# One norm for two, expert gates spread on the chip, and attention layers ended by query halves

## The chip, the cores and the metric

The kernel runs on one core of one Trainium2 chip. The metric is the device time of one execution in microseconds (us); less is better. Five engines work side by side: TensorE (PE; its weight loads are PEld), VectorE (DVE), ScalarE (ACT), GpSimd (POOL) and SyncE (SP), which here only issues DMAs.

## The reference

A stream of 1024 tokens of width 128 passes two layers. Each layer is an attention block over a context of 6404 rows (16 heads of 64), then a block of 8 experts of which each token takes two.

```python
x = x + tanh(g_xattn[0]) * L0_xattn(ctx, layernorm(x), ...)   # normalises its latents once more
x = x + tanh(g_ffn[0])   * L0_ffn(layernorm(x), ...)          # relu experts, 512 wide
x = x + tanh(g_xattn[1]) * L1_xattn(layernorm(x), ctx, ...)   # "stable" norm in and out
x = x + tanh(g_ffn[1])   * L1_ffn(layernorm(x), ...)          # gelu experts, 64 wide

def stable_layernorm(x, g):
    x = x / max(x, axis=-1)
    return (x - mean(x)) * rsqrt(var(x) + 1e-5) * g
```

In layer 0 the attention takes `layernorm(x)` and applies a layer norm with weights to it again. In layer 1 the input is `stable_layernorm(layernorm(x))`, and the attention output passes `stable_layernorm` once more. So both attention inputs are two norms in a row.

## The kernel before

Tokens lie in `X` as 8 tiles of 128 rows. An attention layer runs 8 groups (`NG`) of 2 heads (`GH`). In a group the context comes in chunks of tiles. For each chunk both query halves (n = 0 and 1, 512 queries each) are worked: `score` (PE), `exp` (ACT), `p_low` (DVE, the low part of the probabilities), `mix_high`, `mix_low` and `mix_last` (PE). After a chunk's half, `add_out` (DVE) adds the accumulated output, 128x512 for each of two heads, into `oacc`. Row 127 of `oacc` holds the softmax denominators. The very last unit of the loop is half n = 1 of the last chunk; half n = 0 of `oacc` is complete one unit, some 10 us, earlier.

The order of the work is written out by hand: each engine runs its own program in order, and semaphores join them. A group's output is finished in the group after it, in the shade of the loop: `load_den` (SP) writes the denominator row to DRAM, reads it back spread over partitions, `sum_inverse` (DVE) inverts it, and SP writes it out and broadcasts it into `den`. `o_high` (ACT) and `o_low` (DVE) split `oacc` in two parts, `final` (PE) multiplies by the output weights in four quarters f (head e = f // 2, half n = f % 2), `final_mul` (DVE) applies `den`, `final_add` adds into `YT`. For the eighth group (r = `NG`) there is no loop left, and the same steps run behind it.

After that a second `nc.Block()` turns `YT` back to token rows and adds it to `X`; in layer 1 it divides by the row maximum and applies `layer_norm` first. A block ends with all engines meeting.

The start of layer 1 on PE is in this order: `project_kv(0, 0)`, `transpose_k(0, 0)`, `project_kv(0, 1)`, and only then the transposes of the normed tokens, which wait for `lat_ready`. `project_kv(0, 0)` waits for `wkv_low(0)`, which is DVE work, and DVE's program has it between the first statistics and the first `ln_apply`.

In the last expert block (`moe_layer`, L = 1) `combine` (DVE) makes the gates with tokens on partitions. `turn_combine` (PE) turns them, `save_combine` (SP) writes them to DRAM, and eight DMAs read them back, each row broadcast to 64 partitions of `spread`. DVE multiplies `hid` by `spread`, and PE projects with the result as stationary operand.

## Time and profile before

| | us |
|---|---|
| median of 3 runs | 4258.66 (4256.95 to 4258.74) |
| the profiled execution | 4258.93 |
| its span, first to last instruction | 4257.1 |
| PE busy | 4085.8 (96%) |
| DVE busy | 3369.8 (79%) |
| ACT busy | 3159.8 (74%) |
| mean granted TensorE clock | 0.983 of full |

The span is 1.8 us shorter than the execution's own time. The page's slices of 106 us show PE busy by nine tenths or more in nearly all; the slices at the start, in the middle and at the end, where one layer gives over to the next, show less.

### The profile page before, as it was taken

Reading aid. Unit: us, or ns where it says so; the run is one execution under the profiler, and the core shown is the slowest. Engines: PE = TensorE matmul, PEld = TensorE weight load, DVE = VectorE, ACT = ScalarE, POOL = GpSimd, SP = SyncE. Lnnn points to the kernel's source line nnn. Section 1 sums busy time; section 2 is a strip of 40 time slices with the busy share of each in tenths; the row PEclk is TensorE's granted clock in tenths of the full one; section 3 lists DMA queues with packets and bytes.
Section 4 is the critical chain, followed back from the end, with each engine's and each line's share of the span. In section 5 each row is a group of like instructions: output and inputs, shape, how many; then the busy total and the mean of one; then the engine's idle time right before and its main releaser. Section 6 shows DMA issues by size and latency. Waiting matters only on the chain. (4 is left out here: it accounts for less than half of the span.)

```text
span 4257.1 us, 66053 instructions
## 1 busy us (share of the span) xinstructions
PE 4085.8 (96%) x26167; PEld 2647.6 (62%) x26167; DVE 3369.8 (79%) x5206; ACT 3159.8 (74%) x5109; POOL 412.3 (10%) x333
## 2 busy tenths in 40 slices
PE   4999999999999999999989899999999999999996
PEld 3666666666666666666657666666666666666664
DVE  7878888788887888878867778777877777877775
ACT  5888898888988889888854666676767676666662
POOL 4111111111111111111100000000000000000000
PEclk8999999999999999999989899999999999999997
DMA  1000000000000000000012000000000000000001
GB/s 41 1 1 17 1 17 1 1 17 1 17 1 1 17 1 17 1 1 18 1 52 79 1 1 17 1 17 1 17 1 17 1 5 13 1 17 1 15 1 44
DMA packets 30550, 50.24 MB, mean 12 GB/s; under 512 B 9166, under 2 KB 19414, under 8 KB 28182
## 3 DMA queue, kind: packets, MB, share of 16 engines
q1 hardware_dynamic: 28324, 45.85, 3.5%
q8 instruction: 211, 3.46, 0.3%
q14 instruction: 93, 0.76, 0.1%
q10 hardware_dynamic: 1922, 0.17, 0.0%
HBM read 45.15 MB, written 0.85 MB: 11 GB/s over the span
## 5 line engine op out<-in xcount | busy, mean ns | idle before, releaser
L819 DVE TENSOR_TENSOR a_probs_lo<-a_probs 128x1024 fp32r<-128x1024 f32 x1760 | 2126.5, 1222 | 562.2 <-ACT a_probs L595 254.6
L591 ACT ACTIVATE a_probs<-scores_ps,a_c_bias,a_k_rstd 128x512 f32<-128x512 f32 x1888 | 1311.9, 776 | 31.3 <-PE scores_ps L1248 30.8
L1273 PE MATMUL out_ps<-a_probs_lo,a_v 128*128 128x512 f32 x3520 | 1134.4, 443 | 0.0
L1266 PE MATMUL out_ps<-a_probs,a_v 128*128 128x512 bf16 x3520 | 952.5, 390 | 17.6 <-DVE a_out_acc L832 17.6
L595 ACT ACTIVATE a_probs<-scores_ps,a_c_bias 128x1024 f32<-128x1024 f32 x816 | 867.6, 1112 | 114.0 <-PE scores_ps L1248 113.3
L1273 PEld LDWEIGHTS out_ps<-a_probs_lo,a_v 128*128 128x128 f32 x3520 | 658.0, 188 | 218.6
L1248 PE MATMUL scores_ps<-a_q_hi,a_k_hi 64*128 64x512 f32 x3520 | 790.4, 444 | 3.1 <-ACT a_probs L591 1.6
L1248 PE MATMUL scores_ps<-a_q_lo,a_k_hi 64*128 64x512 f32 x3520 | 700.9, 392 | 0.0
L1248 PE MATMUL scores_ps<-a_q_hi,a_k_lo 64*128 64x512 f32 x3520 | 697.3, 390 | 0.0
L1266 PEld LDWEIGHTS out_ps<-a_probs,a_v 128*128 128x128 f16 x3520 | 272.2, 96 | 560.5 <-issue 303.0
L560 ACT ACTIVATE a_v<-proj_ps 128x256 f16<-128x256 f32 x448 | 172.2, 384 | 488.9 <-PE proj_ps L1171 488.6
L487 POOL TENSOR_TENSOR a_k_rstd<-a_k_stat,minus_half 128x4 f32<-128x4 f32 x240 | 322.3, 1343 | 1617.4 <-DVE a_k_stat L796 1617.4
L1248 PEld LDWEIGHTS scores_ps<-a_q_hi,a_k_hi 64*128 64x128 f32 x3520 | 332.1, 184 | 192.6 <-issue 87.6
L832 DVE TENSOR_TENSOR a_out_acc<-out_ps,a_out_acc 128x512 f32<-128x512 f32 x576 | 370.4, 685 | 80.5 <-PE out_ps L1273 79.3
L1248 PEld LDWEIGHTS scores_ps<-a_q_lo,a_k_hi 64*128 64x128 f32 x3520 | 335.1, 185 | 74.2
L1248 PEld LDWEIGHTS scores_ps<-a_q_hi,a_k_lo 64*128 64x128 f32 x3520 | 334.7, 186 | 37.4
L571 ACT ACTIVATE a_k_hi<-proj_ps 128x256 fp32r<-128x256 f32 x448 | 172.3, 385 | 238.2 <-PE proj_ps L1179 237.8
L1171 PE MATMUL proj_ps<-a_wkv_hi,a_x_hi 128*128 128x256 f32 x896 | 260.0, 290 | 28.3 <-DVE a_k_lo L811 16.8
L1256 PE MATMUL spare_ps<-a_probs,a_v_last 128*32 128x512 bf16 x3520 | 282.1, 394 | 0.0
L577 ACT ACTIVATE a_v<-a_v 128x512 fp32r<-128x512 f16 x448 | 280.5, 626 | 0.0
L1171 PE MATMUL proj_ps<-a_wkv_lo,a_x_hi 128*128 128x256 f32 x896 | 254.6, 284 | 0.0
L1171 PE MATMUL proj_ps<-a_wkv_hi,a_x_lo 128*128 128x256 f32 x896 | 252.3, 282 | 0.0
(299 smaller groups left out, 3286.2 us busy)
## 6 DMA issues: line engine op xcount, KB each, us to landing
a_den<-a_inv_row SPq DMA_DIRECT2D x16, 1024.0 KB, 4.9
normed<-in_L_xattn_we_g SPq DMA_DIRECT2D x16, 256.0 KB, 2.7
m_gate_spread<-m_combine_row SPq DMA_DIRECT2D x8, 512.0 KB, 4.1
a_wkv_raw<-in_L_xattn_wkv_g SPq DMA_DIRECT2D x16, 128.0 KB, 2.0
a_wo_raw<-in_L_xattn_wo_g SPq DMA_DIRECT2D x16, 128.0 KB, 2.0
m_w_raw<-in_L_ffn_w1T SPq DMA_DIRECT2D x8, 256.0 KB, 4.2
m_w_raw<-in_L_ffn_w2T SPq DMA_DIRECT2D x8, 256.0 KB, 4.7
m_gate_spread<-m_combine_row SPq DMA_DIRECT2D x8, 256.0 KB, 5.5
```

Of the source, the lines that this page charges most:

```text
L487: nc.gpsimd.tensor_tensor(krs[:, par, 2 * j:2 * j + 2, :].rearrange("p t h -> p (t h)"), kst[:, 1, :], mhalf[:, 0:2 * GH], ALU.pow).then_i ...
L571: nc.scalar.activation(kh[:, par, 2 * j:2 * j + 2, :], proj[:, 0:2 * P].rearrange("p (t k) -> p t k", k=P), ACT.Copy).then_inc(hi_done, 1)
L577: nc.scalar.activation(v32[:, par, 2 * j:2 * j + 2, :, :].rearrange("p t h k -> p (t h) k"), v16[:, par, 2 * j:2 * j + 2, :, :].rearrange( ...
L591: ins = nc.scalar.activation(probs[:, pb, e * 512:(e + 1) * 512], scores[:, b, e * 512:(e + 1) * 512], ACT.Exp, bias=cbias[:, tile:tile + ...
L595: ins = nc.scalar.activation(probs[:, pb, :], scores[:, b, :], ACT.Exp, bias=cbias[:, 1:2] if last else cbias[:, 0:1])
L819: nc.vector.tensor_tensor(plow[:, idx % NPL, :], probs[:, idx % NB, :], p_hi[:, idx % NB], ALU.subtract).then_inc(plo_ready, 1)
L832: ins = nc.vector.tensor_tensor(oacc[:, e, q], outs[:, e * 512:(e + 1) * 512], oacc[:, e, q], ALU.add)
L1171: last = nc.tensor.matmul(dst, a[:, x], w[:, :].rearrange("p (a c) -> p a c", a=2), start=t == 0 and m == 0, stop=m == 2, skip_group_check ...
L1248: last = nc.tensor.matmul(scores[:, b, e * 512:(e + 1) * 512], kk[r, c % 2, t, :], qq[r, n * 512:(n + 1) * 512], start=m == 0, stop=m == 2)
L1256: last = nc.tensor.matmul(last_ps[j:j + 32, :], vlast[:, c % 2, t, e, 4 - 4 * n:36 - 4 * n], p_hi[:, idx % NB, e * 512:(e + 1) * 512], sta ...
L1266: nc.tensor.matmul(outs[:, e * 512:(e + 1) * 512], v16[:, c % 2, t, e, :], p_hi[:, idx % NB, e * 512:(e + 1) * 512], start=t == 0, stop=False)
L1273: nc.tensor.matmul(outs[:, e * 512:(e + 1) * 512], v32[:, c % 2, t, e, :], plow[:, idx % NPL, e * 512:(e + 1) * 512], start=False, stop=t ...
```

## The change

1. `ln_stats` gets `twice`: in layer 0 the two norms become one, with the variance v replaced by v (1 + eps) + eps². The second statistics, its power on POOL and the second `ln_apply` go.
2. `max_norm` (new) does a layer norm and the division by the maximum as one: it works out the statistics and the maximum of the unchanged rows, and one factor from both. At the start of layer 1 it replaces norm, maximum, division and second norm; it now stands before `wkv_low(0)` and `wq_low(0)` on DVE. At the end of layer 1 it replaces the division and `layer_norm`.
3. The first addition into `YT` becomes a copy (with the bias in layer 0), so POOL no longer clears `Y`.
4. The end of the eighth group goes by halves. For half 0 the denominators take the way through DRAM as before, but of 512 queries and from the moment when half 0 of `oacc` is complete. For half 1, PE takes them out of `oacc` as columns (eight products with eight columns of the identity), DVE inverts the columns, eight transposes spread them over partitions into `outs`, and ACT copies them to `den`. The output weights are split before the last two pairs of the loop. The quarters run in the order f = 0, 2, 1, 3. The closing block is gone; its work stands at the end of the first one, and each half is turned back as soon as it is summed.
5. The last expert block widens the gates on DVE (parts 0, 3) and ACT (parts 1, 2) to `wide`, PE transposes them into PSUM, and DVE multiplies from there in halves. Nine DMAs go. The projection writes to `scores[:, 1]`, after all four transposed parts.

```diff
-            nc.vector.tensor_scalar(stat[:, 3, c + a:c + b], part[:, a:b, 7], LN_EPS, None, ALU.add).then_inc(var_ready, 1)
+        def max_norm(dve, step, x3, dst3, part, var_ready, rstd_ready, n):
+            x, dst = tiles_of(x3), tiles_of(dst3)
+            ln_moments(dve, step, x, 0, QT, part)
+            top, inv, sq = (stat[:, i, 0:QT] for i in range(3))
+            step(nc.vector.tensor_reduce(top, x3[:, :, :], AX.X, ALU.max))
+            step(nc.vector.tensor_tensor(sq, top, part[:, 0:QT, 6], ALU.subtract) if x3 is X else
+                 nc.vector.tensor_copy(sq, top))
+            step(nc.vector.reciprocal(inv, sq))
+            step(nc.vector.tensor_tensor(sq, inv, inv, ALU.mult))
+            step(nc.vector.tensor_tensor(sq, sq, part[:, 0:QT, 7], ALU.mult))
+            nc.vector.tensor_scalar(stat[:, 3, 0:QT], sq, LN_EPS, None, ALU.add).then_inc(var_ready, 1)
+            dve.wait_ge(rstd_ready, n)
+            step(nc.vector.tensor_tensor(stat[:, 0, 0:QT], stat[:, 0, 0:QT], inv, ALU.mult))
+            ln_apply(dve, step, x, dst, 0, QT, part, rstd_ready, n)
...
 # layer 1, start, DVE
-                    ln_stats(dve, lstep, tiles_of(X), 0, QT, B["few"], var_ready)
                     constants()
+                    max_norm(dve, lstep, X, Y, B["few"], var_ready, rstd_ready, 1)
+                    prep_steps.append(lstep.n)
+                    dve.sem_inc(lat_ready, 1)
                     wkv_low(0)
                     wq_low(0)
...
 # end of an attention layer, DVE
+                        if g == NG - 1 and i == NPR - 1:
+                            wo_low(NG)
+                            sum_inverse_half()
+                            for e in range(GH):
+                                o_low_half(0, e)
                         if i in ENDS:
                             add_out(g, s0, *ENDS[i][0])
...
+                o_low_half(1, 0)
+                column_inverse()
+                o_low_half(1, 1)
+                for n in range(2):
+                    for f in (n, 2 + n):
+                        final_mul(NG, f, last_no(f))
+                    for f in (n, 2 + n):
+                        final_add(NG, f, last_no(f))
...
 # the same, PE
+                for f in (0, 2):
                     final(NG, f, None)
+                for e in range(GH):
+                    pe.wait_ge(o_added, NG * NADD + e + 1)
+                    for j in range(4):
+                        last = nc.tensor.matmul(proj[:, (4 * e + j) * 8:(4 * e + j + 1) * 8], oacc[:, e, 512 + j * P:512 + (j + 1) * P],
+                                                ident[:, P - 8:P], start=True, stop=True, skip_group_check=True)
+                    last.then_inc(d_col, 1)
+                final(NG, 1, None)
+                pe.wait_ge(d_inv, 1)
+                for e in range(GH):
+                    for j in range(4):
+                        last = nc.tensor.transpose(outs[:, k * P:(k + 1) * P], inv8[:, k:k + 1].broadcast_to([P, P]), ident[:, :])
+                    last.then_inc(d_spread, 1)
+                final(NG, 3, None)
...
 # the last expert block, PE
+                    hidden(0)
+                    hidden(1)
+                    spread(0)
+                    hidden(2)
+                    spread(1)
+                    hidden(3)
+                    pe.wait_ge(gelu_done, 3)
+                    spread(2)
+                    pe.wait_ge(hg_done, 2)
+                    spread(3)
+                    pe.wait_ge(gelu_done, 4)
```

## Rows read from the trace of the kernel before

**Rows 1.** Layer 1's loop: stretch, PE, PEld, DVE, ACT, POOL busy (x), clock, DMA.
```profile
2400.00:4170.00 1770.00, 1763.19 (x11498) 1131.98 (x11496) 1387.70 (x1911) 1211.17 (x1715) 10.89 (x14) 1.00 0.03 8
```

**Rows 2.** The chain that ended last, its last two pieces: start, us, what.
```profile
4243.49 10.13 PE out_ps L1869 x64
...
4253.64 0.69 DVE residual L1845
```

**Rows 3.** Timeline of DVE at the start: start, us, engine, line, operation, tiles.
```profile
20.01 1.65 DVE L126 BATCH_NORM_STATS2 squares<-normed 128x6 f32<-128x128 f32 x8
...
22.48 0.06 DVE L997 MEMSET a_c_max<- 128x1 f32 x1
...
24.36 2.14 DVE L139 TENSOR_SCALAR normed<-normed,squares,stat 128x128 f32<-128x128 f32 x8 [0.21 <-POOL stat L151]
```

**Rows 4.** Timeline of layer 1's start on DVE, ACT and PE.
```profile
2338.99 0.29 DVE L837 TENSOR_TENSOR a_wkv_lo<-a_wkv_raw,a_wkv_hi 128x128 fp32r<-128x128 f32 x1 [0.95 <-ACT a_wkv_hi L602]
...
2341.63 0.38 ACT L562 ACTIVATE normed<-proj_ps 128x256 f32<-128x256 f32 x1
...
2347.18 0.41 DVE L805 SCALAR_TENSOR_TENSOR a_v<-a_v,proj_ps 128x252 f16<-128x252 f16 x1
...
2349.32 0.58 PE L1171 MATMUL proj_ps<-a_wkv_hi,a_x_hi 128*128 128x256 f32 x1 [0.93 <-DVE a_k_lo L811]
...
2351.43 1.97 PE L1322 MATMUL scores_ps<-identity,branch 128*128 128x128 f32 x8 [0.46 <-DVEq L1080]
```

**Rows 5.** Timeline of DVE at the end of layer 1's attention.
```profile
4171.81 1.29 DVE L832 TENSOR_TENSOR a_out_acc<-out_ps,a_out_acc 128x512 f32<-128x512 f32 x2 [0.59 <-PE out_ps L1273]
...
4177.63 2.36 DVE L819 TENSOR_TENSOR a_probs_lo<-a_probs 128x1024 fp32r<-128x1024 f32 x2 [1.12 <-ACT a_probs L595]
4181.73 1.29 DVE L832 TENSOR_TENSOR a_out_acc<-out_ps,a_out_acc 128x512 f32<-128x512 f32 x2 [1.75 <-PE out_ps L1273]
...
4186.49 0.48 DVE L849 SCALAR_TENSOR_TENSOR a_wo_lo<-a_wo_raw,a_lift_col,a_wo_hi 128x256 fp32r<-128x256 f32 x1
...
4193.31 2.48 DVE L937 TENSOR_TENSOR a_den<-scores_ps,a_den 128x512 f32<-128x512 f32 x4 [6.17 <-DMA a_den<-a_inv_row]
...
4200.58 1.42 DVE L1428 COPY normed<-scores_ps 128x512 f32<-128x512 f32 x2 [2.38 <-PE scores_ps L1411]
...
4203.53 1.22 DVE L1432 TENSOR_TENSOR normed<-normed,stat 128x1024 f32<-128x1024 f32 x1
```

**Rows 6.** The page's DMA issues: count, KB each, us from issue to landing.
```profile
a_den<-a_inv_row SPq DMA_DIRECT2D x16, 1024.0 KB, 4.9
...
m_gate_spread<-m_combine_row SPq DMA_DIRECT2D x8, 512.0 KB, 4.1
```

**Rows 7.** As rows 1, for four microseconds in layer 1's tail.
```profile
4184.00:4188.00 4.00, 0.77 (x2) 0.70 (x3) 3.00 (x4) 2.46 (x5) 0.00 (x0) 0.54 0.02 2
```

**Rows 8.** Timeline of PE: four transposes at the full clock.
```profile
2333.41 0.66 PE L1783 MATMUL scores_ps<-identity,branch 128*128 128x128 f32 x4 [0.67 <-DVE branch L1667]
```

**Rows 9.** Timeline of DVE at the end of layer 0's attention.
```profile
2193.10 2.57 DVE L819 TENSOR_TENSOR a_probs_lo<-a_probs 128x1024 fp32r<-128x1024 f32 x2 [0.97 <-ACT a_probs L591]
2196.87 1.29 DVE L832 TENSOR_TENSOR a_out_acc<-out_ps,a_out_acc 128x512 f32<-128x512 f32 x2 [1.21 <-PE out_ps L1273]
...
2216.47 1.54 DVE L1425 SCALAR_TENSOR_TENSOR residual<-scores_ps,gates,residual 128x512 f32<-128x512 f32 x2 [2.12 <-PE scores_ps L1411]
```

**Rows 10.** Timeline of the last expert block on DVE, ACT and PE.
```profile
4232.03 0.25 DVE L1524 TENSOR_SCALAR m_combine<-m_combine,gates 128x64 f32<-128x64 f32 x1
...
4233.45 1.02 ACT L1827 ACTIVATE m_hidden<-scores_ps 128x1024 f32<-128x1024 f32 x1 [1.23 <-PE scores_ps L1863]
...
4235.08 1.88 PE L1863 MATMUL scores_ps<-normed_T,m_w 128*128 128x512 f32 x4
```

**Rows 11.** PE's instructions of L1869 alone, two stretches: busy, weight loads, clock, DMA.
```profile
4244.00:4248.00 4.00, 4.00 (x21) 4.00 (x20) 0.50 0.96 207
4249.00:4252.00 3.00, 3.00 (x28) 3.00 (x28) 0.97 0.00 0
```

More of the change, by code:

```diff
@@ L121, in flamingo, with ln_moments @@
         few = sqz[:, :, :].rearrange("p t d -> p (t d)")[:, 0:8 * QT].rearrange("p (t k) -> p t k", k=8)
-        def ln_stats(dve, step, x, a, b, part, var_ready, c=0):
+        def ln_moments(dve, step, x, a, b, part):
             for t in range(a, b):
@@ L766, in _ @@
                                 wo_split(g)
+                        if g == NG - 1 and i == NPR - 3:
+                            wo_split(NG)
                         if g < NG - 1:
@@ new lines, in _ @@
+                pe.wait_ge(lo_done, ONE + NG * NI)
+                for e in range(GH):
+                    pe.wait_ge(o_added, NG * NADD + e + 1)
[4 more added lines that the diff above has]
+                final(NG, 1, None)
@@ new lines, in _ @@
+                pe.wait_ge(d_inv, 1)
+                pe.wait_ge(o_added, 2 + NG * NADD)
+                for e in range(GH):
+                    for j in range(4):
+                        k = 4 * e + j
+                        last = nc.tensor.transpose(outs[:, k * P:(k + 1) * P], inv8[:, k:k + 1].broadcast_to([P, P]), ident[:, :])
+                    last.then_inc(d_spread, 1)
+                final(NG, 3, None)
+                for n, dst in enumerate((last_ps, proj)):
+                    pe.wait_ge(f_add, 4 * (NG - 1) + 2 * n + 2)
+                    for t in range(4):
+                        last = nc.tensor.transpose(dst[:, t * P:(t + 1) * P], YT[:, (4 * n + t) * P:(4 * n + t + 1) * P], ident[:, :])
+                    last.then_inc(tr_done, 1)
@@ L1856, in _, with hidden @@
                     router(pe)
-                    for k in range(FC):
+                    def hidden(k):
                         if k >= 2:
                             pe.wait_ge(gelu_done, k - 1)
-                        if k == 3:
-                            turn_combine(pe)
                         for c in range(2):
```

203 lines of the change are left out of this document (110 added, 93 removed).

## Prediction

> **What bounds the kernel now.** I read the page first, for shares and slices, then a table by stretch. In a layer's loop PE is busy for all but 0.4% at the full clock [rows 1]; the change leaves the instructions there as they are but for the last three pairs of the eighth group. So what can be won lies in the seams: the two starts, the two tails and the last expert block, where short steps follow one another over engines and PE mostly waits. I then read each seam's timeline on all engines, since a seam gains only by what its own chain of waits gives up. The chain that ended last shows just the end: the projection of the last experts and the addition after it [rows 2].
>
> A measurement here can tell about 0.2%, 8.5 us, from no change. The sum is made against the profiled execution's 4258.93 us, which is 0.3 above the median of the runs.
>
> **Start of layer 0.** DVE's second statistics begin at 20.01 and end before 22.48; then, after 0.21 us of waiting for POOL, the second application takes 2.14 us [rows 3]. Both go: 2.46 + 0.21 + 2.14 = 4.8 us. DVE works nearly without a break here and the rest of its program follows as before, PE's transposes come right after it, and the context rows had landed by then, so I take all 4.8 as gain. The bounds are 3.5, if a later piece turns out to wait for a load, and 5.3.
>
> **Start of layer 1.** DVE loses a whole norm. The new one is statistics, maximum, five small steps, POOL's power and one application: I get its end at 2344.3, where the old second one ended at 2351.3. That looks like 7 us, and I take nothing of it. `project_kv(0, 0)` waits for `wkv_low`, which moves behind `max_norm`: from 2338.99 to 2344.4. From there PE, ACT and DVE must alternate. From the start of `wkv_low` to the end of ACT's read of the first keys it took 2338.99 to 2342.01, 3.0 us; `v_low` then takes 0.5 (before, DVE did it only at 2347.18, because it was held by the norms); and from the end of `v_low` at 2347.59 to the free PE behind `project_kv(0, 1)`, which starts at 2349.32 and has 1.65 us of products, 3.4 us went by [rows 4]. Sum: 2344.4 + 3.0 + 0.5 + 3.4 = 2351.3. PE's program has the transposes of the tokens behind that; they began at 2351.43 [rows 4]. So they begin where they began. What DVE was late for, PE's order is late for next. Gain 0.1, bounds -1 and +1.5.
>
> **Tail of layer 1, before.** The loop's last products end at 4181.9. DVE adds them until 4183.0, and the copies of the turned result end at 4202.0 [rows 5]. Between stand the splits, 16 products on a PE whose clock had fallen (0.54 granted from 4184 to 4188, mostly the 1.2 GHz level, after PE stood idle) [rows 7], the denominators' way through DRAM, the eight passes of multiplication and addition (2.48 for four, so 0.62 each), a block's end and eight transposes.
>
> **Tail of layer 1, after.** Half 0 of `oacc` is complete at 4173.1, and its sums are back long before DVE ends its last `p_low` at 4180.0 [rows 5]. Then DVE does, in order, `wo_low` (0.48), the reciprocal (0.25) and two half splits (0.62 each), to 4182.0; only then the last `add_out`, 0.3 late, to 4183.3; `o_low_half(1, 0)` to 4183.95. PE goes from its last product straight to f = 0 and 2 (eight products, 1.9 us at the full clock), sixteen instructions for the columns (1.95, bounded by a full transpose's 0.13 each [rows 8] above and 0.9 in all below), f = 1 (0.95), eight transposes (1.1) and f = 3: it ends at 4188.9 and never stands idle long, so I keep the full clock. The column inverse is done at 4186.05, and behind it, on DVE, waits `o_low_half(1, 1)`, to 4186.75.
>
> The broadcast of half 0's inverses can leave at 4182.6 (reciprocal, two small stores with their landing of 1.4 us). It is half of the 1024 KB that take 4.9 us to land; another broadcast, of 512 KB, took 4.1 [rows 6]. I take 4.1, as the size is the same: 4186.7, where DVE comes free anyway. The eight passes end at 4186.75 + 8 x 0.62 = 4191.75; the copy of half 0 (0.71) is done while PE turns half 1 (0.66 [rows 8]), and the second copy ends at 4193.25. Gain 4202.0 - 4193.25 = 8.75.
>
> The Trainium skill speaks against the idea that half the bytes take half the time: its page DMA: Bandwidth & Descriptors, section Anatomy of one DMA, puts a fixed cost of about 2.0 us on each DMA whatever its size. The rows agree that it is far from half (4.9 against 4.1). By that page an estimate for the half is 2.0 + (4.9 - 2.0)/2 = 3.45 us, and the sum would be 0.5 us lower in layer 0's tail and the same in layer 1's, where DVE is the later one.
>
> The norm behind it gives up the pass of 1.22 us; maximum and reciprocal together took 4202.0 to 4203.53, so a small step is 0.25 or so [rows 5], and four are added (copy, square, product, scale). Net 0.35 less. Tail of layer 1: 9.1, bounds 5 (the clock falls during the columns, and each wait costs more) and 10.5.
>
> **Tail of layer 0.** The same, with three differences. DVE's last `p_low` ends at 2195.67 [rows 9], and the weight split that ACT now does ahead of the last exponentials makes that about 0.4 later; with 1.95 us of new work before it the last `add_out` starts at 2198.05, not at 2196.87 [rows 9], 1.2 late. PE's chain is as long as above and ends at 2204.5. The broadcast lands at 2202.85, the eight passes end at 2207.8, and `X` is complete at 2209.3; it was at 2218.0 [rows 9], where a pass for the bias also stood. Gain 8.7, bounds 5 and 10.
>
> **Last expert block.** The first two hidden parts and the gates don't move in it: gates ready at 4232.3, hidden(1) done at 4233.45, clock full from there [rows 10]. A hidden part is four instructions, 1.7 us (1.88 with the end of the last) [rows 10]; eight transposes 1.1 [rows 8]. PE's list is then spread 0, hidden 2, spread 1, hidden 3, spread 2 and 3: 4233.5 + 1.1 + 1.7 + 1.1 + 1.7 + 1.1 + 1.1 = 4241.3. ACT's two copies of 1.02 fit between its Gelus, DVE's multiplications (eight of 0.69) are ahead of PE all along. The projection starts at 4241.3; it started at 4243.49 [rows 2], a gain of 2.2 only. But PE is not idle ahead of it any more. Before, it ran its first 5 us at the low level, 0.19 us an instruction (21 in 4.0), and the rest at 0.107 (28 in 3.0) [rows 11]. At the latter, 64 take 6.85 instead of 10.1: 3.3 more. Gain 5.5, bounds 0 and 6.5.
>
> **Sum.** 4.8 + 0.1 + 8.7 + 9.1 + 5.5 = 28.2 us. 4258.93 - 28.2 = 4230.7; against the median 4230.4. The cleared `Y` and the gates' DMAs were hidden and count nothing.
>
> **Rivals.**
> - *PE's order at the start of layer 1 does not bind*, and the norm pays its 7 us: 4223.5. For it: DVE is the engine without breaks there. Against: the 3.4 us that follow `v_low` are on PE, ACT and DVE in turn [rows 4]. 7%.
> - *The tails pay half.* DVE, with its new work in front of the last `add_out` and `o_low_half(1, 1)` behind the column inverse, falls behind PE, or the columns, which keep few of PE's cycles busy, let the clock fall and f = 1, the transposes and f = 3 take twice as long: some 3.5 us less in each tail, 4237.5. 18%.
> - *The clock falls in the last block.* Its PE work now comes in short groups with waits between them. If the projection runs at the low level, it costs 64 x 0.195 = 12.5 instead of 6.85, and the block gains nothing: 4236. 13%. The Trainium skill, TensorE: Matmul & The Clock Gate, section A second HAM failure mode, says that such short idles between groups can make the clock go up and down; the trace has fast groups only after 4232, and cannot say.
> - *The new order does not do what it says*: the half-0 chain waits for the end of the loop after all, each tail gains just the closing block, some 4 us: 4240. 4%.
> - *Slower.* The loops lose clock. The seams save 28 us; every us of PE work at the low level in a loop costs one more, so from 28 us of such work the change is even, and with 37 us more it is slower by over 0.2%. For it: PE is the loops' bound, so nothing would hide it. Against: the loop of layer 1 has 1.00 granted throughout [rows 1], and its instructions stay. 3%.
> - The forecast: 55%.
>
> **Numbers.** The forecast's own range is 4226 to 4234. The first rival lies below, three above; from 4223.5 to 4240.5 over 8 in 10 are held, with the bounds of the tails and of the last block inside. Faster by over 0.2% (below 4250.1): 94%, same 3%, slower 3%.
>
> **What the profile after would show.** Layer 0's first transposes 5 us earlier; layer 1's still some 16 us after its block began, with DVE free before them; in the tails PE's products within half a microsecond of the loop's end at 0.39 us each, not 0.63; `X` complete 11.5 us after layer 1's last product plus the norm; in the last block 64 projections at about 0.107 us from start to end. Wrong I would be if the lat transposes of layer 1 came 7 us earlier, or if PE's clock read 0.5 in the last ten microseconds.

## The result and the profile after

The changed kernel takes 4229.89 us, the median of 4 runs (4228.58 to 4231.46); the kernel before, run beside it, 4258.45. The ratio is 0.9934, with a 95% interval from 0.9921 to 0.9946. The forecast was 4230.4. The profiled execution took 4228.58, its span is 4226.8, and the mean granted clock 0.987.

To see where the 30 us between the two profiled executions went, I cut both at the same events: the first exponential of each layer, the end of the last product of weights and values (L1357, L1273 before), and the additions that complete the residual. "Transposes" is the time from the complete residual to the token transposes of layer 1.

| stretch, us | before | after | gained | forecast |
|---|---|---|---|---|
| to layer 0's first exponential | 83.43 | 79.46 | 3.97 | 4.8 |
| loop of layer 0 | 2113.64 | 2114.27 | -0.63 | 0 |
| tail of layer 0, to the residual | 20.94 | 12.56 | 8.38 | 8.7 |
| first expert block | 116.86 | 116.45 | 0.41 | 0 |
| start of layer 1, transposes | 16.56 | 16.46 | 0.10 | 0.1 |
| start of layer 1, first exponential | 33.77 | 30.62 | 3.15 | 0.1 |
| loop of layer 1 | 1813.29 | 1812.88 | 0.41 | 0 |
| tail and norm of layer 1, to the residual | 31.87 | 22.65 | 9.22 | 9.1 |
| last expert block | 40.53 | 35.13 | 5.40 | 5.5 |

Without the row of the transposes, which is a part of the next, the gains make 30.31 us. The last stretch ends with the last addition; the 2.76 us behind it, with the DMA of the output, are the same in both.

The end of the chain, in the changed kernel's chain of waits: start, us, what. The 64 products of the projection take 7.16 us and not 10.13 [rows 2], and PE works from 4199.05 on without a wait that the chain shows.

```profile
4199.05 3.58 PE proj_ps L1558 x16
4202.63 6.58 PE scores_ps L1937 x8
4209.21 0.44 PE proj_ps L1944 x4
...
4216.15 7.16 PE scores_ps L1962 x64
4223.31 0.02 issue
4223.33 0.69 DVE residual L1920
```

The start of layer 0, timeline of DVE, to be held against [rows 3]. The second statistics and the second application are gone; but the rows of the context, on which the statistics ahead of this wait, landed 0.91 us later than in the trace of before, and two memsets come with gaps of 0.18 and 0.49.

```profile
14.22 3.19 DVE L126 BATCH_NORM_STATS2 a_out_acc<-a_probs 128x6 f32<-128x128 f32 x16 [3.99 <-DMA a_probs<-in_ctx]
...
18.75 2.14 DVE L160 TENSOR_SCALAR normed<-residual,squares,stat 128x128 f32<-128x128 f32 x8
21.06 0.06 DVE L1067 MEMSET a_c_max<- 128x1 f32 x1 [0.18 <-DVE normed L160]
21.61 0.17 DVE L1069 MEMSET a_den<- 2x128 f32 x1 [0.49 <-issue]
...
23.27 4.19 DVE L160 TENSOR_SCALAR a_probs<-a_probs,a_out_acc,stat 128x128 f32<-128x128 f32 x16
```

The tail of layer 1, timeline of DVE, where [rows 5] stood. After the last `add_out` there are two waits, 1.69 us for the columns and 0.16 us for the broadcast, and then DVE works to the second copy, which ends at 4177.53, 11.29 us after the last product (20.07 before).

```profile
4166.05 1.29 DVE L881 TENSOR_TENSOR a_out_acc<-out_ps,a_out_acc 128x512 f32<-128x512 f32 x2
4167.44 0.69 DVE L978 TENSOR_TENSOR a_o_lo<-a_out_acc,a_o_hi 128x512 fp32r<-128x512 f32 x1
4169.82 0.21 DVE L986 RECIPROCAL a_q_stat<-proj_ps 128x8 f32<-128x8 f32 x1 [1.69 <-PE proj_ps L1487]
...
4170.75 1.29 DVE L1001 TENSOR_TENSOR a_den<-scores_ps,a_den 128x512 f32<-128x512 f32 x2 [0.16 <-DMA a_den<-a_inv_row]
4171.95 1.48 DVE L1012 TENSOR_TENSOR branch<-branch,a_den 128x512 f32<-128x512 f32 x2
...
4176.84 0.69 DVE L1228 COPY normed<-proj_ps 128x512 f32<-128x512 f32 x1 [0.22 <-PE proj_ps L1502]
```

The tail of layer 0: PE, SyncE's queue and DVE (three timelines). The columns take 1.85 us, as I had them (1.95). The broadcast is issued at 2195.22, 2.3 us behind the first of the two small stores and not 1.9, as in the sum; DVE, which waits 1.16 us for it, goes on 4.08 us after its issue.

```profile
2195.50 1.85 PE L1487 MATMUL proj_ps<-identity,a_out_acc 128*128 128x8 f32 x16
...
2192.92 1.11 SPq L499 DMA_DIRECT2D a_inv_row<-a_sums  x2
2195.22 0.39 SPq L503 DMA_DIRECT2D a_den<-a_inv_row  x1
...
2199.30 1.29 DVE L1001 TENSOR_TENSOR a_den<-scores_ps,a_den 128x512 f32<-128x512 f32 x2 [1.16 <-DMA a_den<-a_inv_row]
```

The start of layer 1, timeline of PE, where [rows 4] stood. The first product waits 11.18 us, in the end for `wkv_low`, as I had said, and the transposes follow 6.1 us later. What I had not said is the last row: the 24 products of the query projection, of which this is one, follow one another at 0.11 us.

```profile
2333.12 0.55 PE L1253 MATMUL proj_ps<-a_wkv_hi,a_x_hi 128*128 128x256 f32 x1 [11.18 <-DVE a_wkv_lo L887]
...
2337.76 0.58 PE L1253 MATMUL proj_ps<-a_wkv_hi,a_x_hi 128*128 128x256 f32 x1 [0.93 <-DVE a_k_lo L860]
...
2339.20 1.91 PE L1406 MATMUL scores_ps<-identity,branch 128*128 128x128 f32 x8
...
2342.13 0.27 PE L1273 MATMUL out_ps<-a_wq_lo,a_ln_hi 128*128 128x128 f32 x1
```

### The profile page after: what moved, and what is told of

Same layout as the page of the kernel before. It is cut to its first block and busy times, and to the rows that moved or that the text cites. A ratio compares the mean times of both kernels' runs of the same rounds, so it can differ in the third digit from the quotient of the medians.

```text
span 4226.8 us, 66167 instructions
## 1 busy us (share of the span) xinstructions
PE 4083.2 (97%) x26246; PEld 2646.0 (63%) x26246; DVE 3359.2 (79%) x5172; ACT 3166.7 (75%) x5119; POOL 408.0 (10%) x329
## 5 line engine op out<-in xcount | busy, mean ns | idle before, releaser
L1357 PE MATMUL out_ps<-a_probs_lo,a_v 128*128 128x512 f32 x3520 | 1134.4, 443 | 0.0
L1357 PEld LDWEIGHTS out_ps<-a_probs_lo,a_v 128*128 128x128 f32 x3520 | 658.0, 188 | 218.7
```

Source lines behind the costliest of these rows:

```text
L1357: nc.tensor.matmul(outs[:, e * 512:(e + 1) * 512], v32[:, c % 2, t, e, :], plow[:, idx % NPL, e * 512:(e + 1) * 512], start=False, stop=t ...
```

## The experiments

Each run was profiled too, and cut as above. Their stretches in us; a run's place in the text says what was edited. "First" is layer 0's first exponential; "transposes" and "start 1" count from the complete residual to the token transposes and to the first exponential of layer 1; "tail 1" has the norm in it. The stretches are of the one execution that was profiled, the median is over all executions of the run.

| run | median | first | tail 0 | transposes | start 1 | tail 1 | last block |
|---|---|---|---|---|---|---|---|
| before | 4258.45 | 83.43 | 20.94 | 16.56 | 33.77 | 31.87 | 40.53 |
| after | 4229.89 | 79.46 | 12.56 | 16.46 | 30.62 | 22.65 | 35.13 |
| old last block | 4235.73 | 79.56 | 12.72 | 16.46 | 30.99 | 22.97 | 39.90 |
| old block, products added | 4232.55 | 79.24 | 12.86 | 16.47 | 30.98 | 22.68 | 38.59 |
| old tails | 4245.35 | 79.19 | 21.05 | 16.42 | 31.07 | 31.37 | 34.30 |
| products added at the end | 4229.85 | 79.47 | 11.88 | 16.47 | 33.33 | 23.40 | 33.06 |
| weight parts early | 4226.03 | 79.44 | 12.80 | 13.47 | 27.90 | 22.65 | 34.28 |
| and tokens first | 4226.41 | 79.20 | 12.08 | 9.76 | 30.14 | 22.79 | 34.28 |
| and products added | 4226.93 | 79.17 | 12.90 | 9.77 | 30.33 | 22.96 | 34.28 |
| reciprocal early | 4226.58 | 79.06 | 11.12 | 16.45 | 30.82 | 22.85 | 34.28 |
| weight parts and reciprocal | 4227.24 | 79.25 | 11.58 | 13.48 | 30.34 | 22.85 | 34.28 |
| reciprocal, new key order | 4228.15 | 79.25 | 11.58 | 9.78 | 30.60 | 22.77 | 34.28 |
| and products in every wait | 4226.64 | 79.32 | 11.56 | 9.77 | 30.59 | 22.39 | 33.80 |
| after, once more | 4228.83 | 79.60 | 12.35 | 16.46 | 33.31 | 23.16 | 34.28 |

The four rows from "old last block" to "products added at the end" were timed beside runs of the kernel before with a median of 4259.08, the next four beside 4257.19, the last four beside 4258.25.

One thing has to be known before two numbers of the column "start 1" are compared. The 24 products of the query projection took 2.9 to 3.05 us, with the clock up from their start or from at most 0.35 us behind it, in the six rows "after", "old last block", "old block, products added", "old tails", "weight parts early" and "reciprocal early". In the other eight, "before" among them, they took 5.38 us, all at 0.50. Only rows of the same level can be compared.

**The last expert block undone.** All its edits are taken back, the rest stays.

```diff
-                    for k in (0, 3):
-                        nc.vector.tensor_copy(wide[:, k], gates_of(k)).then_inc(wide_ready[k], 1)
+                    dve.wait_ge(ct_done, ONCE)
+                    nc.vector.tensor_copy(combT[:, :], proj[0:QT * NE, 0:P]).then_inc(ct_read, 1)
...
+                            sp.dma_start(spread[i * FH:(i + 1) * FH, c, :],
+                                         comb_row[2 * c + i:2 * c + i + 1, :].partition_broadcast(FH)).then_inc(g_all[c], 16)
```

> The changed kernel with the last expert block alone as it was: combine transposed, written to device memory and read back as eight broadcasts, one gating multiply per expert pair of 1024 columns. If the block is worth what its stretch of the two traces says (residual complete to last vector operation 40.53 us before, 35.13 after), this runs 5.4 us longer than the changed kernel, at about 4235.3, and its projection of 64 products takes about 10.1 us because the granted clock is back at 0.50 when it begins. Rival: the block's gain was partly a gift of the shorter tail ahead of it (the phase of the clock); then the old block behind the new tail takes another length than 40.5 us and the difference is not 5.4.

4235.73 us, ratio 0.9946 (0.9929 to 0.9962): 5.8 more than the changed kernel's median, and 5.2 more if each is taken against the kernel before that ran beside it (23.4 us faster in place of 28.6). The block took 39.90 against 34.28 to 35.13 in the unedited new one: 4.8 to 5.6 us. The expected 5.4 holds; the rival has a little of it, as the old block behind the new tail took 0.6 less than in the kernel before. The projection began with the clock low again, but rose earlier and took 8.90, not 10.1. Timeline of PE and the wait ahead of it:

```profile
4221.16 8.90 PE L1937 MATMUL out_ps<-m_w,m_hidden 128*128 128x128 f32 x64 [6.46 <-DVE m_hidden L1909]
```

**Products added to the old block's wait.**

```diff
+    for j in range(5):
+        nc.tensor.matmul(spare[:, 0:512], ident[:, :], lnT[:, 0:512], start=True, stop=True, skip_group_check=True)
     for k in range(FC):
         pe.wait_ge(hg_done, k + 1)
```

> As the run with the old last expert block, with five products of 128x512 added on TensorE in its wait for the gate broadcasts, into a PSUM bank that the block does not use. They add no result. At 0.86 us each at full clock they fill 4.3 of the 6.5 us of that wait. My theory has 3.3 of the block's 5.4 us come from the clock: then the 64 products of the projection take about 7 us in place of 10.1, and the run is about 3 us shorter than the one without the added products, at about 4232. Rival: the projection was slow for another reason, as waiting on VectorE's multiplies expert pair by expert pair; then it is not shorter by more than 0.5 us, or longer if the added products run into the projection.

The run came out 3.2 us shorter, as my theory said, and for another reason. The added products filled 4.46 us, the wait shrank to 2.28, and the projection took 9.04: no faster than without them. What made the block 1.3 us shorter was its hidden part (6.83 for 12 instructions against 8.41), in which nothing was edited: the clock rose to full there at another moment. The rest of the difference between the two traces lies ahead of the block, 0.95 of it in the loop of layer 0. The table by stretch of this run (length, PE, PEld, DVE, ACT and POOL busy, clock, DMA) shows the clock at full through the added products and the wait, and falling only when the projection was under way:

```profile
4214.00:4216.00 2.00, 1.82 (x5) 0.51 (x3) 0.00 (x0) 0.00 (x0) 0.00 (x0) 1.00 1.04 240
4216.00:4218.00 2.00, 0.00 (x0) 0.00 (x0) 1.18 (x1) 0.00 (x0) 0.00 (x0) 1.00 1.03 229
4218.00:4220.00 2.00, 1.90 (x14) 1.90 (x15) 1.00 (x2) 0.00 (x0) 0.00 (x0) 0.86 1.04 231
4220.00:4222.00 2.00, 2.00 (x12) 2.00 (x10) 0.97 (x2) 0.00 (x0) 0.00 (x0) 0.50 1.00 225
4222.00:4224.00 2.00, 2.00 (x16) 2.00 (x16) 1.09 (x2) 0.00 (x0) 0.00 (x0) 0.79 0.06 12
```

So filling two thirds of the wait did not spare the projection. That the projection's own products are faster at the full clock is seen in the changed kernel (7.3 us in every trace); that it was the missing wait that kept the clock there remains argued, not shown. A median alone would have confirmed me wrongly here.

**The old tails, with the new norms and the new last block.** Both attention layers end with the closing block as before.

```diff
-                    step(nc.vector.tensor_reduce(stat[:, 0, 0:QT], Z[:, :, :], AX.X, ALU.max))
-                    step(nc.vector.reciprocal(stat[:, 1, 0:QT], stat[:, 0, 0:QT]))
-                    step(nc.vector.tensor_tensor(Z[:, :, :], Z[:, :, :], over(stat[:, 1, 0:QT], full), ALU.mult))
-                    layer_norm(dve, step, Z, Z, QT, var_ready, rstd_ready, 3)
+                    max_norm(dve, step, Z, Z, B["few"], var_ready, rstd_ready, 2)
```

(against the kernel before; the rest of the closing block is that kernel's)

> The kernel before with the new norms and the new last expert block, and both attention layers ending as before with a closing block. It leaves out the tails only. The tails measured 8.4 us (layer 0) and 8.8 us (layer 1) between the two traces, so by my reading this runs 17.2 us longer than the changed kernel, at about 4247. Rival: the tails' gain overlaps with that of the blocks that follow them (their first instructions waited for something else); then it is nearer to 4240. Rival: the changed layer 1 start owes its 3.1 us to the phase of the clock and not to the norm; then the start of layer 1 in this trace, with the same instructions but 8.4 us later in the run, shows the clock at 0.50 to the end of the query projection, and the run is up to 3 us longer still.

4245.35 us, ratio 0.9971 (0.9958 to 0.9983), 15.5 more than the changed kernel (14.8 against the kernels before beside each). The traces give 8.5 us for tail 0 and 8.7 for tail 1, 17.2 as expected; 1.9 of it is made up by small differences of the other stretches (0.57 and 0.24 in the loops, 0.83 in the last block). The tails' gain does not overlap with that of the blocks behind them. The rival about the start of layer 1 is not settled by this trace: 31.07 us, but its query projection ran at the full clock (2.90 us), as in the first trace of the changed kernel. The traces with that projection at the low level decide it, and for the rival: 33.33 in the next run and 33.31 in the last, against 33.77 before. Of the 3.15 us of the first trace, then, some 0.5 are the change's and the rest the clock's.

**Products added at the end of the changed kernel.** The first ten stand behind the last transposes of attention layer 1, the six ahead of the transposes of the last expert block.

```diff
+    for j in range(10):
+        nc.tensor.matmul(scores[:, 1, 0:512], ident[:, :], YT[:, 0:512], start=True, stop=True, skip_group_check=True)
...
+    for j in range(6):
+        nc.tensor.matmul(outs[:, 0:512], ident[:, :], Y[:, 0:4, :].rearrange("p t d -> p (t d)"),
+                         start=True, stop=True, skip_group_check=True)
     pe.wait_ge(z_ready, ONCE)
```

> The changed kernel with 16 products of 128x512 that add no result, on TensorE where it only waits for norms: ten behind the last transposes of attention layer 1 and six at the start of the last expert block. In the trace of the changed kernel the clock is 1.00 to the end of the tail (4178) and 0.50 from 4196 to about 4208.6, where the transposes take 1.97, the router 3.58 and the first two hidden products 6.73 us. If the clock is what makes them long, they take about 1.0, 1.8 and 3.5 us and the run is 5 to 6 us shorter, at about 4224. Rival: the waits ahead of them keep them from moving, or the vector chain top two, exponential, combine is the one that ends last; then the hidden products get faster but the first spread waits for the combine weights as before and no more than about 3 us come out. Against it: the added products could delay the real ones if the clock falls regardless, up to 4 us longer.

4229.85: no gain in the median, where I had expected 5 to 6 us; the rival was nearer. The last block did take 2.1 us less than in the first trace of the changed kernel (33.06 against 35.13), but tail 1 took 0.75 more, and the start of layer 1, far ahead of the edit, 2.7 more. Timeline of PE: the transposes ran fast (1.10), the router 3.24 and the first hidden products 5.73 mostly slow, since the clock fell at about 4201.7, behind two waits of 1.1 us. And the vector chain from the norm to the widened gates (`m_gate_wide`) is close behind PE there: in six traces of the new block PE waits for that copy (0.1 to 0.6 us), the first spread begins 19.24 to 19.25 us after the complete residual, and the block takes 34.28. The first trace of the changed kernel, with 20.15 and 35.13, is the only one in which the hidden products ended clearly later. So faster hidden products alone could give 0.9 us against that trace, and nothing against the others. Timeline of PE in the last run below, the changed kernel once more:

```profile
4213.00 0.66 PE L1944 MATMUL proj_ps<-identity,m_gate_wide 128*128 128x128 f32 x4 [0.41 <-DVE m_gate_wide L1910]
```

Timeline of PE in this run:

```profile
4192.54 5.39 PE L1929 MATMUL out_ps<-branch,identity 128*128 128x512 f32 x12 [1.68 <-PEq L428]
4199.07 1.10 PE L1932 MATMUL scores_ps<-identity,normed 128*128 128x128 f32 x8 [1.14 <-DVEq L1908]
4201.28 3.24 PE L1561 MATMUL proj_ps<-m_wg,normed_T 128*128 128x8 f32 x16 [1.11 <-ACT normed_T L1894]
```

**The weight parts made during the root.** This tests the step by which I had taken nothing for the shorter norm of layer 1. `max_norm` calls the two functions ahead of its wait for the root.

```diff
-max_norm(dve, lstep, X, Y, B["few"], var_ready, rstd_ready, 1)
+max_norm(dve, lstep, X, Y, B["few"], var_ready, rstd_ready, 1, (wkv_low, wq_low))
...
-wkv_low(0)
-wq_low(0)
```

> The changed kernel with one thing moved: at the start of attention layer 1 the low parts of the first key/value and query weights are made on VectorE while it waits for GpSimd's root (1.8 us idle in the changed trace), not behind the eight tile multiplications of the norm. My prediction held that the order of TensorE's work binds there (product, transpose of keys, product, then the tokens), and so that a shorter norm is worth 0.1 us. If so, the first product begins about 3.5 to 4.3 us earlier after the residual is complete (6.1 us after it in place of 10.4), the second is then held by the keys' chain behind the norm (about 3.1 us earlier), the token transposes begin about 13.3 us after the residual in place of 16.5, and the first exponential comes about 3 us earlier at an equal clock. Rival: the tokens or ScalarE bind behind it, and the first exponential moves by less than 1 us. The clock of that start was low to 2348 in one trace (33.3 us from the residual to the first exponential) and to about 2342 in four (30.6 to 31.1); the comparison takes the state of the clock into account.

The transposes came 13.47 us after the residual and not 16.46, the first exponential 27.90 and not 30.62; the run took 4226.03, ratio 0.9927 (0.991 to 0.9944). PE's first product began 5.9 us after the residual, then its second waited for the keys' chain. So PE's order does bind there. Both first exponentials are of the full clock. At the low level the same edit (the run with the reciprocal, below) gives 30.34 in place of 33.31 and 33.33: 2.7 and 3.0 us. The times alone don't show it, since the interval overlaps with that of the changed kernel. Timelines of DVE and PE:

```profile
2328.59 0.28 DVE L888 TENSOR_TENSOR a_wkv_lo<-a_wkv_raw,a_wkv_hi 128x128 fp32r<-128x128 f32 x1
...
2330.61 0.17 DVE L155 TENSOR_TENSOR stat<-stat 128x8 f32<-128x8 f32 x1 [1.33 <-POOL stat L174]
...
2336.77 1.91 PE L1406 MATMUL scores_ps<-identity,branch 128*128 128x128 f32 x8
```

**The tokens ahead of the second key product**, on PE as the diff shows, and on ScalarE and VectorE in the same sense.

```diff
                     project_kv(0, 0, 0, None)
-                    transpose_k(0, 0)
-                    project_kv(0, 1, 0, None)
                     for i, (kind, tiles, at) in enumerate(jobs):
...
-                    transpose_k(0, 1)
+                    transpose_k(0, 0)
                     for b in range(2):
                         pe.wait_ge(tr_read, b + 1)
                         project_q(0, b, None)
+                    project_kv(0, 1, 0, None)
+                    transpose_k(0, 1)
```

> As the run with the weight parts moved into the wait for the root, and with the token transposes and the query projection of attention layer 1 ahead of the second key/value product on TensorE, ScalarE and VectorE. If TensorE's order binds, the token transposes begin as soon as the norm ends, about 9.8 us after the residual in place of 16.5, and the first exponential comes 5 to 7 us earlier than in the changed kernel: the run at about 4224. Rival: the second and third key items, now later, end last (the first score waits for the first item alone, the third waits for more): then it is no better than the run with the moved parts, about 4227. The clock can add up to 3 us to either.

The transposes came where I expected them, 9.76 us after the residual, and yet the first exponential came after 30.14 us, 2.2 later than with the weight parts alone. The clock was at 0.50 until 2347 in this trace, so the 24 products of the query projection took 0.21 us each. At that level the run with the weight parts and the reciprocal took 30.34, so the new order was worth 0.2 us at most and not 2 to 4. The rival about the later key items may be the reason; this run does not show it.

**With added products ahead of the first one.**

```diff
+for j in range(11):
+    nc.tensor.matmul(scores[:, 1, 0:512], x_hi[:, 0:P], x_hi[:, 0:512], start=True, stop=True,
+                     skip_group_check=True)
 project_kv(0, 0, 0, None)
```

> As the run with the new order at the start of layer 1, with eleven products of 128x512 in the reduced type added on TensorE ahead of its first product, where it has nothing to do for 5 us. They add no result. The clock is 0.50 there and rises in the middle of the query projection. If earlier work brings the rise forward, the 24 products of the query projection take 0.11 us each, the whole start takes 1 to 3 us less than in the run without them. The trial with added products in the last block speaks against much: there the clock fell at 4202 behind 20 us that were nearly filled, and began to rise again at 4208. Then nothing is gained, and if the added products last longer than the wait, up to 0.5 us is lost.

30.33 us. The added products did bring the clock up (table by stretch, below): the first key product ran at 0.12 us an instruction. Then PE waited 2.45 us for the norm, and the query projection ran at the low level as without them.

```profile
2326.00:2328.00 2.00, 2.00 (x7) 1.52 (x6) 1.86 (x5) 0.82 (x3) 0.00 (x0) 0.50 0.20 32
2328.00:2330.00 2.00, 2.00 (x11) 1.72 (x9) 0.84 (x5) 0.00 (x0) 1.57 (x1) 0.77 0.06 19
2330.00:2332.00 2.00, 0.21 (x2) 0.01 (x1) 1.76 (x8) 0.66 (x2) 0.30 (x3) 1.00 0.25 79
2332.00:2334.00 2.00, 1.34 (x7) 1.34 (x8) 1.03 (x5) 0.13 (x1) 0.00 (x0) 0.58 0.00 0
2334.00:2336.00 2.00, 1.57 (x8) 1.17 (x7) 1.32 (x2) 1.90 (x4) 0.00 (x0) 0.50 0.00 0
```

**The reciprocal of the half sums earlier.**

```diff
 if g == NG - 1 and i == NPR - 1:
     wo_low(NG)
-    sum_inverse_half()
...
+if g == NG - 1 and i == NPR - 2:
+    sum_inverse_half()
 if more:
     p_low(s0, 2 * i + 3)
```

> The changed kernel with the reciprocal of the first query half's sums taken between the last two low parts of the weights, 1.6 us earlier than now in either layer; so the stores of the inverse and the broadcast into den are issued earlier. In the changed trace VectorE waits 1.16 us (layer 0) and 0.16 us (layer 1) for that broadcast at its first multiplication. If nothing else is late there, the tail of layer 0 (last product to complete residual, 12.56 us) gets 1.2 us shorter, that of layer 1 0.2 us: about 1.3 us in all. Rival: the sums have not landed when the reciprocal is due, it holds the last low part back, and the product behind it with it: then the loop's end is later by what the tail gains.

Tail 0 took 11.12 us, 1.4 less than in the changed kernel's first trace, and DVE no longer waited for the broadcast; tail 1 did not gain (22.85). Over all traces with the new tails, tail 0 lies between 11.88 and 12.90 without this edit (eight traces, the mean is 12.5) and between 11.12 and 11.58 with it (four), so the broadcast that ended last there costs about 1 us. The landing of that broadcast accounts for most of the spread: in the three of the eight traces where it came 3.5 us after the issue, tail 0 took 11.88 to 12.35, in the five with 3.8 to 4.0 us 12.56 to 12.90. Nothing was held back: the loop of layer 0 took 2114.06. The median, 4226.58 (ratio 0.9931, 0.9914 to 0.9948), cannot show so little.

**The edits together, and a new order of the key items.** Four kernels beside one another.

> The changed kernel with two edits that each had a run: weight parts in the wait for the root, and the reciprocal of the half sums two instructions earlier. By the traces, 2.7 us out of the start of layer 1 (30.62 to 27.90) and 1.4 out of the tail of layer 0 (12.56 to 11.12), about 4 us together: 4226. If the two only trade with the clock's phase they don't add, and it is no better than the run with the first alone.

> As the run of those two, and with the new order at the start of layer 1 in which the third key item no longer stands ahead of the norm bound on VectorE (in the trace with the tokens first, its low part waited for a product that began 22.5 us after the residual, and the first exponential came 30.1 us after it though the tokens were turned 6.7 us earlier). Now the third item's product follows the bound, and its transposes and splits follow the first scores and the first exponential. If that queue was what ended last, the first exponential comes 25 to 27 us after the residual and the run is 1 to 3 us shorter than the one with the two edits, at 4223 to 4225. Rival: the key items then are late for the scores of the loop's first steps, and the loop takes longer by what the start gains.

The second kernel's new order on VectorE; on TensorE the third item's product follows the bound, and its transposes the first two scores:

```diff
-                    v_low(0, 2)
                     norm_max(0, 1, 1)
...
                     bound_everywhere()
-                    k_low(0, 2)
                 bias_new(0)
+                if L == 1:
+                    v_low(0, 2)
+                    k_low(0, 2)
```

> As the run before it, with added products that give no result on TensorE from the last product of attention layer 1 to the router of the last expert block, now in every wait on the way: one behind the last final product, one between the transposes of the two halves, eleven behind them, six at the start of the expert block, one ahead of the router. In the earlier trial the clock fell to 0.50 at 4178, in a wait of 3 us ahead of the added products, and again at 4202 between two waits of 1.1 us. If the waits are what lets it fall, it stays at 1.00 to the end here: router 1.8 in place of 3.6, hidden products 3.4 in place of 6.7, and the last block takes 3 to 4 us less than its 34 to 35. If the clock falls with no regard to such work, the block takes 33 to 35 us as before and the tail up to 1 us more.

> The changed kernel once more, as the measure for the three others on the same chip: 4228 to 4231. Its segments should be those of the first trace but for the clock's phase: 30.6 to 31.1 us (clock up in the query projection) or about 33.3 (clock low) from the residual to the first exponential of layer 1.

| run | median | runs from to | ratio to before, interval |
|---|---|---|---|
| weight parts and reciprocal | 4227.24 | 4221.92 to 4227.54 | 0.9922 (0.9909 to 0.9936) |
| reciprocal, new key order | 4228.15 | 4226.85 to 4228.78 | 0.9929 (0.9916 to 0.9943) |
| and products in every wait | 4226.64 | 4226.01 to 4227.72 | 0.9926 (0.9911 to 0.9941) |
| after, once more | 4228.83 | 4227.38 to 4232.67 | 0.9930 (0.9916 to 0.9943) |

The intervals overlap: none of the three is shown to beat the changed kernel. The first had the start of layer 1 at 30.34 us, although its transposes came as early as in the run with the weight parts alone (13.48, and there 27.90): the difference of 2.4 is again the query projection, at 0.50 from 2338 to 2344 (11 instructions in 2 us). The second did not get its 25 to 27 us: 30.60, though the third key item was out of the way. Its DVE waited 5.51 us for ScalarE's read of the second item, which I had put behind the query's squares and which the multiplication for the bound stood behind (timeline of DVE). My theory of the queue was blind to that item. But it explains only a part: the squares that the multiplication reads were complete on ScalarE at 2339.57, so the place of the item cost it 2.1 us, and the longer part of the wait is the query projection, again at the low level (5.38 us).

```profile
2341.23 0.17 DVE L857 SCALAR_TENSOR_TENSOR a_v_last<-a_v,proj_ps 128x4 f16<-128x4 f16 x1 [5.51 <-ACT normed L602]
2341.31 0.41 DVE L859 SCALAR_TENSOR_TENSOR a_v<-a_v,proj_ps 128x252 f16<-128x252 f16 x1
2341.64 1.22 DVE L1164 TENSOR_TENSOR a_den<-squares,a_rows 128x1024 f32<-128x1024 f32 x1
```

The third kept the clock at 1.00 through the tail, lost it at the seam of the blocks, at about 4189.7, behind a wait of 3.24 us, and had it back by 4194. Against the second kernel the router took 1.95 in place of 3.58 and the first hidden products 3.68 in place of 5.70, 3.65 us less together, but the last block took only 0.5 us less. Timeline of PE: the spreads now wait 1.98 us for the vector chain (top two, exponential, combine, wide copy), which ends last, and behind that wait, at about 4206.7, the clock falls again, so hidden 2 takes 3.58 and not 1.88.

```profile
4198.34 1.95 PE L1575 MATMUL proj_ps<-m_wg,normed_T 128*128 128x8 f32 x16 [0.25 <-ACT normed_T L1908]
4200.15 3.68 PE L1961 MATMUL scores_ps<-normed_T,m_w 128*128 128x512 f32 x8
4205.81 0.66 PE L1968 MATMUL proj_ps<-identity,m_gate_wide 128*128 128x128 f32 x4 [1.98 <-DVE m_gate_wide L1927]
...
4206.74 3.58 PE L1961 MATMUL scores_ps<-normed_T,m_w 128*128 128x512 f32 x4
```

The fourth, the changed kernel once more, shows what moves when nothing is edited. Against the trace of before it gained 3.8 us to the first exponential of layer 0, 8.6 in tail 0, 0.5 in the start of layer 1, 8.7 in tail 1 and 6.25 in the last block, and lost 1.3 and 0.4 in the loops. Its start of layer 1 took 33.31 us; the transposes came after 16.46, to the hundredth as before. Table by stretch, first its own rows in the query projection, then those of the first trace at the same place (its residual was complete 0.9 us earlier):

```profile
2342.00:2344.00 2.00, 1.57 (x8) 1.17 (x7) 1.93 (x5) 1.48 (x3) 0.00 (x0) 0.50 0.01 4
2344.00:2346.00 2.00, 2.00 (x11) 2.00 (x11) 0.87 (x5) 0.30 (x1) 0.00 (x0) 0.50 0.00 0
```

```profile
2340.00:2342.00 2.00, 1.57 (x9) 1.14 (x7) 1.33 (x4) 1.64 (x5) 0.00 (x0) 0.61 0.00 0
2342.00:2344.00 2.00, 2.00 (x18) 2.00 (x19) 1.83 (x8) 1.07 (x3) 0.00 (x0) 1.00 0.01 4
```

The same instructions in the same order, eleven of them in two microseconds at 0.50 and eighteen at 1.00.

## Why the prediction was right, step by step

**The sum.** 28.2 us forecast; 28.6 between the medians, 30.3 and 26.3 between the trace of before and the two of the changed kernel. That the median came within 0.5 us is in part luck: I had priced no difference of the clock from one execution to the next, and it moved the start of layer 1 by 2.7 us and the last block by 0.85. The four times of the changed kernel lie in two pairs (4228.58 and 4228.69, 4231.08 and 4231.46); whether these are the two levels is not shown, as only the first has a trace. The rival with 18%, that the tails pay half, is excluded by the traces and by the run with the old tails.

**Start of layer 0.** Right in what goes, 0.8 too much in size: 3.97 in the first trace, and 3.8 to 4.4 over all thirteen with the new norm. In the first trace 0.9 us went to the later landing of the context rows and 0.5 to two gaps, so DVE came to the norm's application to the context (23.27, before 26.66) 3.4 us earlier: the case of my lower bound. What gave 0.6 back ahead of the first exponential stays open.

**Start of layer 1.** The step "PE's transposes begin where they began" was met to 0.15 us in seven traces (16.42 to 16.47 against 16.56), and the run with the weight parts shows that it is `wkv_low`'s new place behind the norm that costs: 3.0 us came back at once. What failed is the step behind it, that with the transposes the rest stays where it was too. In five of those seven traces the first exponential came after 30.6 to 31.1 us, in the other two after 33.3, and before after 33.8: two levels some 2.5 us apart, set by whether the clock has risen by the start of the query projection or rises behind it (2.9 to 3.05 us for its products, or 5.38). The rows by stretch in the last experiment show it. Before, the projection was at the low level too; compared at that level, the start gained 0.44 and 0.46, inside my bounds. I had priced no clock there, and the first trace was 3 us better than my sum at this place: that is nearly all the clock and not the norm, and only one trace of the kernel before exists to say how often it was high there.

**Tails.** 8.4 and 9.2 against 8.7 and 9.1. PE's columns (1.85 for 1.95) were as taken. From the last product to the end of the second copy layer 1 took 11.29 us (11.32 in my sum), and the norm gave up 0.44 (0.35). In tail 0 the broadcast ended last, as forecast. From issue to landing it took 4.0 us there and 3.5 in tail 1, and 3.4 to 4.0, 3.7 in the mean, over the 24 of all traces with the new tails; I had taken 4.1. The estimate from the Trainium skill, DMA: Bandwidth & Descriptors, section Anatomy of one DMA, was 3.45 us for the broadcast; that section is on DMAs that GpSimd issues, and these are issued by SyncE. The traces have values on both sides of it, so here the nearest row was no better a guide than the page: one was the upper end, the other near the lower. The first expert block's broadcasts of the same size have a median of 4.0.

**Last block.** 5.40 against 5.5, and 5.8 between the medians with the block undone. Within the first trace three errors met. The clock rose later in the block, at 4208.6, so hidden 1 ended 13.2 us after the block's transposes began (4195.97) and not 12.6 (4220.89 to 4233.45 [rows 10]). And eight spreads took 0.88 us and not 1.1, four times, so the projection began 6.9 us after hidden 1 and not 7.8. The projection itself gave 3.0 us and not 3.3 (7.16 in the chain, 6.85 in my sum). In the eight other traces without edits to the block the clock rose earlier in it, and it took 34.28 to 34.30, a gain of 6.2: 0.7 more than the forecast. In six of them the vector chain was the last that the spreads waited for; I had it 1.2 us ahead of hidden 1 (gates at 4232.3) and left it out, with the copy to `wide` behind it. The projection took 7.31 us in all eleven traces of the new block, clock at full, and 8.90 to 10.11 in the three of the old one. The rival with 13%, which the Trainium skill (TensorE: Matmul & The Clock Gate, section A second HAM failure mode) spoke for, did not come in the change as made; with all waits filled the clock did go down and up within the block (0.50 from about 4206.7 to 4210.1), once.

**The loops.** 0 forecast; -0.63 and +0.41 measured. Over all traces, the loop of layer 0 took 2113.6 to 2115.0 us and that of layer 1 1812.6 to 1814.0, the kernel before among them, so neither is a gain or a loss of the change.

## What to carry over

Price a seam by its two halves: what the shorter chain releases first (here the product that PE's order puts ahead), and at which level of the clock the work behind it will run; the second was worth 2.5 to 2.7 us and I had left it out. Cut two traces at the same events and add up the stretches before believing a median: one run here gave the expected 3 us, and none of it came from the projection that the edit was for. Filling PE's waits with spare products paid in none of the four kernels here: it moved the moment at which the clock changes, and the gain ended at the next wait or the next engine.

## What the runs showed that I had not expected

In the start of layer 1 the clock rose 3.7 us after the second product had begun in one trace of the changed kernel (2337.76, rise at about 2341.5) and 11.7 us after it in the other (2338.63, rise at about 2350.3), with PE busy 9.6 of the 10 us ahead of the later rise. In the old block with products added, PE kept the full clock through a wait of 2.28 us and lost it after work had begun again. And real work that began 6.7 us earlier (transposes 9.76 in place of 16.46) came out 0.5 us ahead at the first exponential of the first trace, 3.2 ahead of the one with the low clock. What decides between the two levels in that start stays open; the two traces of one kernel show only that it is not the instructions or their order alone.
